# The first expert layer's weight splitting moved into the cross attention; bias two tiles ahead on GpSimd, context copies on ScalarE

## The chip, the cores and the metric

One Trainium2 chip, one of its cores. The metric is the device time of one execution in microseconds (us), the median of several; the profile is one further execution, recorded by the hardware profiler. The engines: TensorE (PE in the rows, its weight loads PEld), VectorE (DVE), ScalarE (ACT), GpSimd (POOL) and SyncE (SP), which issues DMAs.

## The reference, cut to what matters

```python
# two layers over x of 32 x 64 tokens, width 256; the change touches two steps of the first
x = x + L0_attn(layernorm(x), ...)                    # rotary recurrence
x = x + L0_xattn(layernorm(x), ctx, ctx, mask, ...)   # cross attention
x = x + L0_ffn(layernorm(x), ...)                     # 16 routed experts, top 2, and 2 shared
x = x + L1_attn(...); x = x + L1_xattn(...); x = x + L1_ffn(...)

def L0_xattn(query, key, value, mask, Wq, Wk, Wv, Wo):       # 16 heads of 16, 4 kv heads
    scores = einsum(Q / 4, K) + slope * (k - q)
    scores = where(mask, scores, finfo.min)
    return softmax(scores) @ V @ Wo

def L0_ffn(x, wa, rg, rgb, rw1, rb1, rw2, rb2, sg, sgb, sw1, sb1, sw2, sb2):
    aff = sigmoid(x @ wa); p, i = top_k(aff, 2); p = p / sum(p)
    expert(e) = (gelu(x @ g[e] + gb[e]) * (x @ w1[e] + b1[e])) @ w2[e] + b2[e]
    return x + sum over the 2 chosen of p * expert_r + sum over both shared of expert_s
```

## The kernel before, in words

The program is a row of stages, each an instruction block with a barrier at its end: load, rotary recurrence, cross attention, first experts, lightning attention, quantised attention, second experts. Within a block the order of each engine's instructions is written out by hand, and semaphores join them.

**Cross attention** (`gqa_cross_attention`, tag b). 2048 tokens are 16 tiles of 128, in 4 groups of 4 (a hardware loop `Fori(0, NBLK)`). A group begins with the projections of its 512 tokens: TensorE makes Q (L721) in two banks and K (L725), ScalarE copies them out (QT L604, Kbd L607), TensorE makes V from `ctxS` (L733), a copy of the group's context rows that GpSimd made with `tensor_copy` (L591); ScalarE copies V out (L613). Then for each tile: TensorE scores (L697); VectorE's `front`: scores times 1/4 plus bias (L651, two halves), row maximum (L656), subtract it (L657); ScalarE exp (L624); VectorE row sum (L672) and reciprocal (L673), then the front of the next tile; TensorE transposes (L745), ScalarE copies them out (PT L627), TensorE mixes V (L755); VectorE scales by the reciprocal (ao L677); TensorE transposes ao (L707), ScalarE copies it (aoT L618, `ao_copy`), TensorE multiplies by Wo (L715), VectorE adds to X (L662). GpSimd makes the `bias` of tile n, alibi plus mask (L595), in two buffers. `biased` starts at 2, so tiles 0 and 1 are made at once; the bias of tile n + 2 waits for the front of tile n to have read its buffer, and the next group's ctxS stands between.

**First experts** (`experts_top2`, tag c). TensorE works in fp16 pairs: each of the 18 experts' weights, scaled by 1024, is split in a high and a low half. SP loads gate, up (128x512 together) and down (128x256) of an expert into one of 6 staging slots (L1177, L1179; six experts ahead of the constants, two between the transposes, the rest when slots come free), ScalarE scales in place (L1256, L1257) and rounds to the high half (L1259, L1260), GpSimd subtracts for the low half (L1230, L1231). Beside it the layernorm runs (`RowNorm`: bn_stats L875, square root on ScalarE L905, reciprocal L880, normalise L893, add to X L898, high half on ScalarE L909, low half on VectorE L885), SP transposes each of 4 blocks (L918) and keeps its rows in memory (L919), TensorE makes the router's logits, and VectorE the routing (`Dispatch`: L1007 to L1107: choice, positions, one-hot tables, the list of tokens by expert). GpSimd gathers the rows by that list (L1240), SP transposes them (L1207), TensorE runs the experts over 12 quads, then the two shared experts; results go to memory (`y_dram`) and GpSimd gathers them back (L1248) in 8 slots G, which VectorE adds to X (L1353). ScalarE's queue has two splits ahead of the square root, one after each block's high half, two ahead of the router's weights (L984), and ten after the scores; SP's has two weight loads ahead of block 2's transpose. A stage of its own (`m.stage()`) clears the semaphores at its end.

Of the kernel before, what the change touches and what calls it, by code (L numbers as in the profile page):

```python
# [530 lines left out]
def gqa_cross_attention(nc, m, w):  # L531
# [10 lines left out]
    with ExitStack() as own:  # L542
# [12 lines left out]
        neg = sb("neg", [P, NT, SEQ])  # L555
# [11 lines left out]
        def preload(sp):  # L567
            def load(dst, src):
                sp.dma_start(dst, src).then_inc(loaded, 16)
            with nc.allow_non_contiguous_dma("small weights, mask rows"):  # L570
# [9 lines left out]
                for b in range(2):  # L580
                    src = w["mask_BxS2_bf1"].rearrange("(t b) k -> b t k", b=2)[b]
                    load(mask8[b * SEQ:(b + 1) * SEQ, :, :], src.partition_broadcast(SEQ))

        layernorm(nc, m, preload)
        with nc.Block() as block:
            @block.gpsimd
            def _(pool):
                pool.wait_ge(prep, 1 + KC * C)
                with pool.Fori(0, NBLK) as i:
                    pool.wait_ge(proj, i * 4 + 4)  # L590
                    pool.tensor_copy(ctxS[:, :, :], m.ctxT[:, :, ds(i * BLK, BLK)]).then_inc(ctx_copied, 1)  # L591
                    for tt in range(TPB):
                        n = i * TPB + tt
                        pool.wait_ge(biased, n + 1)
                        pool.tensor_tensor(bias[:, tt % 2, :, :], alibi[:, :, :],  # L595
                                           neg[:, ds(n, 1), :].broadcast_to((P, NH, SEQ)), ALU.add).then_inc(bias_ready, 1)

            @block.scalar
            def _(act):
                act.wait_ge(prep, 1 + KC * C)  # L600
                with act.Fori(0, NBLK) as i:
                    for c in range(2):
# [18 lines left out]
                    for tt in range(TPB):  # L621
# [7 lines left out]
                        if tt:  # L629
                            ao_copy(n - 1)  # L630
                    ao_copy(i * TPB + TPB - 1)

            @block.vector
            def _(dve):
                dve.wait_ge(loaded, 16 * NLOAD)
                dve.tensor_scalar(neg[:, :, :], mask8[:, :, :], 1.0, FLT_MAX, ALU.subtract, ALU.mult).then_inc(prep, 1)
# [50 lines left out]
            def _(pe):  # L687
                pe.wait_ge(prep, 1 + KC * C)
# [421 lines left out]
def experts_top2(nc, m, w, rows_dram, y_dram):  # L1110
# [8 lines left out]
    ORDER = [*range(NE + SH)]  # L1119
    STAGES, GOT, TURNED, GSLOTS = 6, 2, 3, 8  # L1120
    HS = 256.0
    shared_steps = SH * NBLK
    (scaled, high, split, hhigh, hlow, loaded, gate_up, gated, hready, downs, summed, bias_high, bias_split, bias_moved, bias_clear,
     tables, table_in, evac_act, evac_dve, combined) = (m.sem(f"c_{n}") for n in (
        "scaled", "high", "split", "hhigh", "hlow", "loaded", "gate_up", "gelu", "h", "downs", "summed", "bias_high",
        "bias_split", "bias_moved", "bias_clear", "tables", "table_in", "evac_act", "evac_dve", "combined"))
    w_in = [m.sem(f"c_w{i}") for i in range(STAGES)]
# [4 lines left out]
    with ExitStack() as own:  # L1132
# [24 lines left out]
        src_r = {"Wg": w["L0_ffn_rg"], "Wu": w["L0_ffn_rw1"], "Wd": w["L0_ffn_rw2"]}  # L1157
        src_s = {"Wg": w["L0_ffn_sg"], "Wu": w["L0_ffn_sw1"], "Wd": w["L0_ffn_sw2"]}
# [6 lines left out]
        with nc.Block() as block:  # L1165
            @block.sync
            def _(sp):
# [3 lines left out]
                def weights(n):  # L1171
                    if n >= STAGES:
                        sp.wait_ge(split, n - STAGES + 1)
                    e, slot = ORDER[n], n % STAGES
                    src, e = (src_r, e) if e < NE else (src_s, e - NE)
                    for part, name in enumerate(("Wg", "Wu")):
                        sp.dma_start(Wgu[:, slot, :, part, :],  # L1177
                                     src[name][e].rearrange("(k p) f -> p k f", p=P)).then_inc(w_in[slot], 16)
# [1277 lines left out]
```

## Time and profile before

| | |
|---|---|
| median of 3 runs | 2751.41 us (2748.73 to 2751.82) |
| profiled execution, its own time | 2745.09 us |
| its span, first to last instruction | 2743.3 us |
| mean granted TensorE clock | 0.794 |
| busy in the span | PE 74%, DVE 63%, ACT 52%, POOL 37% |
| DMA | 135.44 MB, mean 49 GB/s |
| cross attention | about 277 to 476 us |
| first experts | about 476 to 707 us |

Rows in order of time have the start, the busy time, the engine, the line, the operation with output and inputs, and in brackets the engine's idle time before it and who ended that. Groups have the count, busy time and mean. A line's number is that of the kernel before. Granted clock is in parts of 2.4 GHz.

### The profile page before, as it was taken

To read this page: it belongs to the slowest core of one execution; us is meant where nothing else is said; L and a number is where in the kernel's file an instruction comes from. 1 tells how busy PE (TensorE), PEld (TensorE's weight loads), DVE (VectorE), ACT (ScalarE), POOL (GpSimd) and SP (SyncE) were. 2 spreads that over 40 slices of the span, in tenths; PEclk is the share of its full clock that TensorE was granted. 3 is DMA by queue.
4 is the path that set the end of the run, shared out by engine and by line. 5 is a ranking of instruction groups with operands and counts; after the bars stand their busy time and mean duration, and the time that the engine had idled before them with its cause. 6 is when DMAs were issued, how large, how long until landed. Compare 5 with 4: busy or idle time off the path is not lost. (4 is left out here: it accounts for less than half of the span.)

```text
span 2743.3 us, 44098 instructions
## 1 busy us (share of the span) xinstructions
PE 2041.8 (74%) x15822; PEld 1216.7 (44%) x15822; DVE 1739.4 (63%) x3149; ACT 1419.1 (52%) x1986; POOL 1017.3 (37%) x920
## 2 busy tenths in 40 slices
PE   6784777168499999999764466666666549999998
PEld 3332555056377777777554122222222334444444
DVE  5997465724533333333456899999999645666665
ACT  4562332522333333333232688888888416666664
POOL 0000221653332232223233788888888500101010
PEclk9996877589799999999877555555555559999999
DMA  2000000675100000000000456666566300000001
GB/s 92 0 0 20 1 0 9 159 175 134 52 20 20 19 10 19 19 19 10 24 0 0 77 106 107 108 107 107 108 107 107 58 18 18 17 26 17 26 17 40
DMA packets 374723, 135.44 MB, mean 49 GB/s; under 512 B 317549, under 2 KB 371525, under 8 KB 374597
## 3 DMA queue, kind: packets, MB, share of 16 engines
q1 hardware_dynamic: 370757, 123.27, 21.4%
q0 software_dynamic: 3840, 10.49, 1.6%
q8 instruction: 79, 1.29, 0.2%
q14 instruction: 47, 0.39, 0.0%
HBM read 47.69 MB, written 10.49 MB: 21 GB/s over the span
## 5 line engine op out<-in xcount | busy, mean ns | idle before, releaser
L2021 POOL CAST xnT<-xl 128x2048 bf16<-128x2048 uint8 x256 | 483.6, 1890 | 15.4
L2056 PE MATMUL psum<-e_KT,e_QT 48*128 48x512 bf16 x1024 | 264.8, 617 | 272.7 <-DVE ctxT L2089 125.3
L2089 DVE TENSOR_SCALAR_CACHE_REDUCE ctxT<-psum,e_nsq 128x1024 f32<-128x1024 f32 x256 | 314.7, 1282 | 11.8 <-PE psum L2056 10.1
L2089 DVE TENSOR_SCALAR_CACHE_REDUCE e_Smore<-psum,e_nsq 128x1024 f32<-128x1024 f32 x256 | 314.7, 1281 | 1.5
L2107 ACT ACTIVATE xh<-e_Smore,e_ebias 128x2048 uint8<-128x2048 f32 x128 | 256.3, 2002 | 48.6 <-POOL e_ebias L2028 48.6
L2107 ACT ACTIVATE xh<-ctxT,e_ebias 128x2048 uint8<-128x2048 f32 x128 | 256.2, 2002 | 47.6 <-POOL e_ebias L2028 47.6
L1569 POOL TENSOR_TENSOR d_sq<-d_oS 128x512 f32<-128x512 f32 x64 | 99.1, 1549 | 420.8 <-ACT d_oS L1613 420.8
L117 PE MATMUL psum<-xh,d_WT 128*128 128x512 f16 x768 | 229.9, 382 | 2.6 <-DVE d_WT L1644 2.6
L2056 PEld LDWEIGHTS psum<-e_KT,e_QT 48*128 48x128 bf16 x1024 | 33.7, 107 | 402.6 <-DVE ctxT L2089 190.6
L1663 DVE TENSOR_TENSOR d_ACC<-psum,d_ACC 128x512 f32<-128x512 f32 x128 | 82.4, 686 | 171.1 <-PE psum L1717 171.1
L2245 POOL TENSOR_TENSOR f_WA<-f_W,f_WA 128x512 f16<-128x512 f32 x17 | 19.6, 1155 | 410.0 <-ACT f_W2H L2265 410.0
L2066 PEld LDWEIGHTS psum<-e_Vi,xnT 128*128 128x128 bf16 x4096 | 119.4, 104 | 112.1 <-issue 104.3
L117 PE MATMUL psum<-xh,f_WA 128*128 128x512 f16 x544 | 154.4, 387 | 13.9 <-DVEq L2300 11.8
L2316 DVE SCALAR_TENSOR_TENSOR X<-psum,f_route,X 128x256 f32<-128x256 f32 x272 | 112.8, 477 | 70.3 <-PE psum L2376 70.3
L2376 PE MATMUL psum<-f_W2H,f_hh 128*128 128x256 f16 x544 | 151.1, 278 | 3.1 <-DVE f_hh L2328 3.1
L2376 PE MATMUL psum<-f_W2L,f_hh 128*128 128x256 f16 (+1 forms) x544 | 150.8, 277 | 0.0
L2066 PE MATMUL psum<-e_Vi,xnT 128*128 128x16 bf16 x4096 | 131.2, 175 | 7.4 <-POOL xnT L2021 7.4
L1657 DVE SCALAR_TENSOR_TENSOR d_y<-d_gt,d_oS 128x512 f32<-128x512 f32 x64 | 44.3, 693 | 145.6 <-ACT d_oS L1613 145.6
L1717 PE MATMUL psum<-d_WoT,d_y 128*128 128x256 f32 x512 | 122.7, 382 | 5.8 <-DVE d_y L1657 5.7
L2279 ACT ACTIVATE f_h<-psum 128x512 f32<-128x512 f32 x68 | 40.6, 597 | 158.8 <-PE psum L117 158.8
L1597 ACT ACTIVATE d_kT<-psum 128x512 f32<-128x512 f32 x64 | 38.2, 597 | 159.3 <-PE psum L117 159.3
L2306 DVE TENSOR_TENSOR f_pr<-psum,f_h 128x512 f32<-128x512 f32 x68 | 47.0, 692 | 111.3 <-ACT f_h L2279 111.3
(364 smaller groups left out, 4682.3 us busy)
## 6 DMA issues: line engine op xcount, KB each, us to landing
kept_y<-c_y SPq DMA_DIRECT2D x12, 512.0 KB, 5.1
d_Wn<-in_L_attn_w_qkv SPq DMA_DIRECT2D x16, 384.0 KB, 3.2
f_W<-in_L_ffn_w_routed SPq DMA_DIRECT2D x32, 176.0 KB, 2.5
xl<-xh SPq DMA_TRANSPOSE x256, 3.0
ctx_rows<-in_ctx SPq DMA_DIRECT2D x1, 2048.0 KB, 8.5
X<-in_x SPq DMA_DIRECT2D x1, 2048.0 KB, 14.0
c_Wgu<-in_L_ffn_rg SPq DMA_DIRECT2D x16, 128.0 KB, 2.7
c_Wgu<-in_L_ffn_rw SPq DMA_DIRECT2D x16, 128.0 KB, 2.8
```

What stands on the lines that cost most here:

```text
L117: mm = pe.matmul(out, lhsT(a, k), rhs(b, k), start=(n == 0), stop=(n == len(terms) - 1))
L1569: pool.tensor_tensor(sq[:, :], o, o, ALU.mult).then_inc(squared, 1)
L1663: last = dve.tensor_tensor(a2, m.bank[6 + half][:, :], a2, ALU.add)
L1717: mm = pe.matmul(m.bank[6 + j // 2][:, (j % 2) * D:(j % 2 + 1) * D], y[:, j * P:(j + 1) * P], WoT[:, slot, :], start=True, stop=True)
L2021: pool.tensor_copy(PT[:, sl, :], P8[:, sl, :, :].rearrange("p c q -> p (c q)").bitcast(U8)).then_inc(unpacked, 1)
L2056: mm = pe.matmul(m.bank[pair_banks(c + odd) + q], QT[rows, n // 2, :], KTt[rows, n % H // 2, col:col + BLK], start=True, stop=True)
L2066: mm = pe.matmul(m.bank[6 + j // 8][:, j % 8 * HD:(j % 8 + 1) * HD], PT[:, n % SLOTS, k // 2 * 2 * P + k % 2:(k // 2 + 1) * 2 * P:2], Vi[: ...
L2089: dve.tensor_scalar(S32[sl][:, hf * HALF:(hf + 1) * HALF].rearrange("p (a b) -> p a b", a=2), m.psum[:, b:b + 2, :], nsq[:, n + odd:n + od ...
L2107: act.activation(e8[:, sl, :], S32[sl], ACT.Exp, bias=ebias[:, sl:sl + 1], scale=-1.0, accum_out=esum[:, n:n + 1]).then_inc(exped, 1)
L2306: dve.tensor_tensor(pr[:, st % 2, 0, :], m.bank[1][:, :], h1[:, st % 2, 0, :], ALU.mult).then_inc(product, 1)
L2316: last = dve.scalar_tensor_tensor(m.X[:, t, :], m.bank[4 + 2 * (q % 2) + j // 2][:, (j % 2) * D:(j % 2 + 1) * D], R.route[:, t, ds(e, 1)], ...
L2376: mm = pe.matmul(m.bank[4 + 2 * (q % 2) + j // 2][:, (j % 2) * D:(j % 2 + 1) * D], a, b, start=(n == 0), stop=(n == len(terms) - 1))
```

## The change

The buffers for staging (4 slots in place of 6) and for the split weights belong to a new class, `SplitWeights`, that lives over both stages, which now share one `m.stage()`. In the attention: the shared experts are loaded with the preload and split ahead of the first group; then one routed expert's split goes with each tile, on ScalarE after the tile's evacuations, on GpSimd ahead of the bias of the tile after the next. GpSimd's bias is made two tiles ahead across groups too (`neg` gets two zero rows for the last two), and its copy of the context goes to ScalarE, ahead of the first QT copy. In the expert stage all loads and splits are gone; the router's weights are rounded after block 0's high half, and the results are gathered in 16 slots laid over xnT.

```diff
+class SplitWeights:
+    NE, SH, F, SLOTS = 16, 2, 128, 4
...
+    def load(self, sp, kind, e, slot):
+        for part, name in enumerate(("g", "w1")):
+            sp.dma_start(self.Wgu[:, slot, :, part, :],
+                         self.w[f"L0_ffn_{kind}{name}"][e].rearrange("(k p) f -> p k f", p=P)).then_inc(self.w_in[slot], 16)
+        sp.dma_start(self.Wd[:, slot, :], self.w[f"L0_ffn_{kind}w2"][e]).then_inc(self.w_in[slot], 16)
+    def scalar(self, act, e, slot, loads, n):
+        act.wait_ge(self.w_in[slot], 48 * loads)
+        act.activation(self.Wgu[:, slot], self.Wgu[:, slot], ACT.Copy, scale=SPLIT)
+        act.activation(self.Wd[:, slot], self.Wd[:, slot], ACT.Copy, scale=SPLIT).then_inc(self.scaled, 1)
+        act.wait_ge(self.scaled, n + 1)
+        act.activation(self.Wx[:, ds(e, 1), 0].rearrange("p o k a f -> p (o k a f)"),
+                       self.Wgu[:, slot].rearrange("p k a f -> p (k a f)"), ACT.Copy)
+        act.activation(self.WdH[:, ds(e, 1)].rearrange("p o d -> p (o d)"), self.Wd[:, slot], ACT.Copy).then_inc(self.high, 1)
+    def gpsimd(self, pool, e, slot, n):
+        pool.wait_ge(self.high, n + 1)
+        flat = lambda x: self.Wx[:, ds(e, 1), x].rearrange("p o k a f -> p (o k a f)")
+        pool.tensor_tensor(flat(1), self.Wgu[:, slot].rearrange("p k a f -> p (k a f)"), flat(0), ALU.subtract)
+        pool.tensor_tensor(self.WdL[:, ds(e, 1)].rearrange("p o d -> p (o d)"), self.Wd[:, slot],
+                           self.WdH[:, ds(e, 1)].rearrange("p o d -> p (o d)"), ALU.subtract).then_inc(self.split, 1)
...
-        neg = sb("neg", [P, NT, SEQ])
+        neg = sb("neg", [P, NT + 2, SEQ])
...
+            for slot in range(W.SH):
+                W.load(sp, "s", slot, slot)
...
+            @block.sync
+            def _(sp):
+                for slot in range(W.SH):
+                    sp.wait_ge(W.split, slot + 1)
+                    W.load(sp, "r", slot, slot)
+                for slot in range(W.SH, W.SLOTS):
+                    W.load(sp, "r", slot, slot)
+                with sp.Fori(1, NBLK) as i:
+                    for slot in range(W.SLOTS):
+                        sp.wait_ge(W.split, i * W.SLOTS + (W.SH - W.SLOTS + 1) + slot)
+                        W.load(sp, "r", i * W.SLOTS + slot, slot)
             @block.gpsimd
             def _(pool):
+                for slot in range(W.SH):
+                    W.gpsimd(pool, W.NE + slot, slot, slot)
...
+                def mask_bias(n, half):
+                    pool.wait_ge(biased, n + 1)
+                    pool.tensor_tensor(bias[:, half, :, :], alibi[:, :, :],
+                                       neg[:, ds(n, 1), :].broadcast_to((P, NH, SEQ)), ALU.add).then_inc(bias_ready, 1)
+                mask_bias(0, 0)
+                mask_bias(1, 1)
                 with pool.Fori(0, NBLK) as i:
-                    pool.wait_ge(proj, i * 4 + 4)
-                    pool.tensor_copy(ctxS[:, :, :], m.ctxT[:, :, ds(i * BLK, BLK)]).then_inc(ctx_copied, 1)
                     for tt in range(TPB):
-                        n = i * TPB + tt
-                        pool.wait_ge(biased, n + 1)
-                        pool.tensor_tensor(bias[:, tt % 2, :, :], alibi[:, :, :],
-                                           neg[:, ds(n, 1), :].broadcast_to((P, NH, SEQ)), ALU.add).then_inc(bias_ready, 1)
+                        W.gpsimd(pool, i * W.SLOTS + tt, tt, i * W.SLOTS + (W.SH + tt))
+                        mask_bias(i * TPB + (tt + 2), tt % 2)
             @block.scalar
             def _(act):
+                for slot in range(W.SH):
+                    W.scalar(act, W.NE + slot, slot, 1, slot)
...
                 with act.Fori(0, NBLK) as i:
+                    act.wait_ge(proj, i * 4 + 4)
+                    act.activation(ctxS[:, :, :], m.ctxT[:, :, ds(i * BLK, BLK)], ACT.Copy).then_inc(ctx_copied, 1)
...
                         if tt:
                             ao_copy(n - 1)
+                        W.scalar(act, i * W.SLOTS + tt, tt, i + (2 if tt < W.SH else 1), i * W.SLOTS + (W.SH + tt))
                     ao_copy(i * TPB + TPB - 1)
...
-    STAGES, GOT, TURNED, GSLOTS = 6, 2, 3, 8
+    GOT, TURNED, GSLOTS = 2, 3, 16
...
-        G = norm.xn[:, :, :, :].rearrange("p a b d -> p (a b) d")
+        G = m.xnT[:, :, :].rearrange("p a b -> p (a b)").rearrange("p (s d) -> p s d", s=GSLOTS)
...
-                    for n in range(STAGES):
-                        weights(n)
...
-                    if b == 1:
-                        weights(STAGES)
-                        weights(STAGES + 1)
-                for n in range(STAGES + 2, NE + SH):
-                    weights(n)
...
-                for n in range(NE + SH):
-                    e, slot = ORDER[n], n % STAGES
-                    pool.wait_ge(high, n + 1)
-                    pool.tensor_tensor(Wx[:, e, 1], Wgu[:, slot], Wx[:, e, 0], ALU.subtract)
-                    pool.tensor_tensor(WdL[:, e], Wd[:, slot], WdH[:, e], ALU.subtract).then_inc(split, 1)
...
-                split_high(0)
-                split_high(1)
                 norm.scalar_sd(act)
-                for b in range(NBLK):
-                    norm.scalar_high(act, b)
-                    split_high(2 + b)
-                split_high(STAGES)
-                split_high(STAGES + 1)
+                norm.scalar_high(act, 0)
                 act.wait_ge(loaded, 16 * NLOADS)
                 act.activation(b2[:, 0, :], b2[:, 0, :], ACT.Copy, scale=HS * SPLIT).then_inc(bias_high, 1)
                 R.scalar_gate(act, R.wa[:, :, :].rearrange("p k e -> p (k e)"))
+                for b in range(1, NBLK):
+                    norm.scalar_high(act, b)
                 R.scalar_scores(act, m.bank[6])
-                for n in range(STAGES + 2, NE + SH):
-                    split_high(n)
...
-                pe.wait_ge(split, NE + SH)
...
-        with m.stage():
-            experts_top2(nc, m, w, kept_rows, kept_y)
+        with m.stage(), ExitStack() as split:
+            W = SplitWeights(m, w, split)
+            gqa_cross_attention(nc, m, w, W)
+            experts_top2(nc, m, w, W, kept_rows, kept_y)
```

## Rows read from the trace of the kernel before

**Rows 1.** Busy time (count) of stretches: length, PE, PEld, DVE, ACT, POOL, granted clock, DMA share, GB/s.
```profile
291.00:340.00 49.00, 36.87 (x324) 27.17 (x324) 28.04 (x32) 15.67 (x25) 11.39 (x5) 0.79 0.00 1
...
476.00:562.00 86.00, 8.05 (x164) 7.18 (x164) 58.70 (x150) 40.20 (x83) 53.99 (x46) 0.51 0.60 152
```

**Rows 2.** Timeline of the first group of the attention, VectorE and GpSimd.
```profile
293.38 2.31 DVE L657 TENSOR_TENSOR b_S<-b_S,b_mx 128x1024 f32<-128x1024 f32 x1
...
299.98 2.36 POOL L595 TENSOR_TENSOR b_bias<-b_alibi,b_neg 128x1024 f32<-128x1024 f32 x1 [5.37 <-DVE b_S L651]
...
301.09 2.33 DVE L657 TENSOR_TENSOR b_S<-b_S,b_mx 128x1024 f32<-128x1024 f32 x1
```

**Rows 3.** Timeline of the attention's last group, VectorE.
```profile
441.41 2.32 DVE L657 TENSOR_TENSOR b_S<-b_S,b_mx 128x1024 f32<-128x1024 f32 x1
...
456.70 1.23 DVE L657 TENSOR_TENSOR b_S<-b_S,b_mx 128x1024 f32<-128x1024 f32 x1
...
463.17 1.22 DVE L657 TENSOR_TENSOR b_S<-b_S,b_mx 128x1024 f32<-128x1024 f32 x1
```

**Rows 4.** Timeline, ScalarE's idle stretches in a tile and between groups.
```profile
313.87 0.39 ACT L618 ACTIVATE b_aoT<-psum 128x256 f32<-128x256 f32 x1
...
318.67 1.06 ACT L624 ACTIVATE b_S<-b_S 128x1024 f32<-128x1024 f32 x1 [4.40 <-DVE b_S L657]
...
332.18 0.60 ACT L604 ACTIVATE b_QT<-psum 128x512 f32<-128x512 f32 x1 [3.14 <-PE psum L721]
...
335.50 2.00 PEld L733 LDWEIGHTS psum<-b_Wv,b_ctxS 128*64 128x64 f32 x64 [0.76 <-issue]
```

**Rows 5.** GpSimd's subtractions by tile, ns min/median/max; ScalarE's splits in the timeline.
```profile
L1230 POOL TENSOR_TENSOR c_Wx<-c_Wgu,c_Wx x18: 1148/1188/3195, 481.9 to 544.5; 128x512 f16<-128x512 f32 x18
...
L1231 POOL TENSOR_TENSOR c_WdL<-c_Wd,c_WdH x18: 661/675/2717, 483.0 to 546.3; 128x256 f16<-128x256 f32 x18
...
521.13 0.61 ACT L1256 ACTIVATE c_Wgu<-c_Wgu 128x512 f32<-128x512 f32 x1
...
522.93 0.62 ACT L1256 ACTIVATE c_Wgu<-c_Wgu 128x512 f32<-128x512 f32 x1
```

**Rows 6.** Head of the experts to the logits: timeline, and groups by line.
```profile
485.25 0.25 DVE L880 RECIPROCAL c_rstd<-c_sd 128x16 f32<-128x16 f32 x1 [2.82 <-ACT c_sd L905]
...
485.54 1.38 DVE L893 TENSOR_SCALAR c_xn<-X,c_mom,c_rstd 128x256 f32<-128x256 f32 x4
...
L893 DVE TENSOR_SCALAR c_xn<-X,c_mom,c_rstd 128x256 f32<-128x256 f32 x16 | 8.1, 569 | 0.1
...
L885 DVE SCALAR_TENSOR_TENSOR xnT<-c_xn,xnT 128x1024 f16<-128x1024 f32 x4 | 5.7, 1458 | 0.0
...
508.66 3.54 SPq L918 DMA_TRANSPOSE xl<-xnT  x1
...
514.91 0.81 PE L117 MATMUL psum<-c_wa,xl 128*128 128x16 f16 x24 [1.75 <-DMA xl<-xnT]
```

**Rows 7.** Routing: groups by line, a short one of the later experts, the first gather.
```profile
L1053 DVE TENSOR_TENSOR c_base<-c_upto,c_need 128x16 f32<-128x16 f32 x1 | 1.1, 1120 | 0.0
...
L1089 DVE TENSOR_TENSOR c_tilehot<-c_iota,c_tile 128x768 f16<-128x768 f32 x2 | 3.3, 1633 | 0.0
...
L1091 DVE TENSOR_TENSOR c_tilehot<-c_tilehot,c_tokid 128x768 f16<-128x768 f16 x2 | 3.1, 1549 | 0.1
...
L1093 DVE TENSOR_TENSOR c_y<-c_iota,c_row 128x2048 f16<-128x2048 f32 x2 | 6.0, 2992 | 0.0
...
L828 DVE TENSOR_SCALAR f_tot<-f_tot 128x16 f32<-128x16 f32 x1 | 0.2, 175 | 0.0
...
549.16 1.30 POOL L1240 DMA_INDIRECT xnT<-kept_rows,c_token  x1 [2.20 <-DVE c_token L1107]
```

**Rows 8.** End of the stage: the last gather, the next stage's first instruction.
```profile
703.22 0.95 POOL L1248 DMA_INDIRECT c_xn<-kept_y,c_home  x1 [0.30 <-issue]
...
711.93 0.06 DVE L183 MEMSET ln_eps<- 128x1 f32 x1 [5.47 <-PEq L87]
```

More of the change, by code:

```diff
@@ L528, in _, with __init__, gqa_cross_attention @@
                 output(NBLK - 1)
-def gqa_cross_attention(nc, m, w):
+class SplitWeights:
+    NE, SH, F, SLOTS = 16, 2, 128, 4
+    def __init__(self, m, w, own):
+        NE, SH, F, SLOTS = self.NE, self.SH, self.F, self.SLOTS
+        self.w = w
+        self.Wgu = m.sb("c_Wgu", [P, SLOTS, KC, 2, F], ctx=own)
+        self.Wd = m.sb("c_Wd", [F, SLOTS, D], ctx=own)
+        self.Wx = m.sb("c_Wx", [P, NE + SH, 2, KC, 2, F], F16, own)
+        self.WdH, self.WdL = (m.sb("c_" + n, [F, NE + SH, D], F16, own) for n in ("WdH", "WdL"))
+        self.scaled, self.high, self.split = (m.sem(f"c_{n}") for n in ("scaled", "high", "split"))
+        self.w_in = [m.sem(f"c_w{i}") for i in range(SLOTS)]
+    def load(self, sp, kind, e, slot):
[17 more added lines that the diff above has]
+                           self.WdH[:, ds(e, 1)].rearrange("p o d -> p (o d)"), ALU.subtract).then_inc(self.split, 1)
+def gqa_cross_attention(nc, m, w, W):
     G, C, HD = 4, 4, 16
@@ L635, in _ @@
                 dve.wait_ge(loaded, 16 * NLOAD)
-                dve.tensor_scalar(neg[:, :, :], mask8[:, :, :], 1.0, FLT_MAX, ALU.subtract, ALU.mult).then_inc(prep, 1)
+                dve.memset(neg[:, NT:, :], 0.0).then_inc(prep, 1)
+                dve.tensor_scalar(neg[:, 0:NT, :], mask8[:, :, :], 1.0, FLT_MAX, ALU.subtract, ALU.mult).then_inc(prep, 1)
                 for k in range(KC):
@@ L1169, in load @@
                     sp.dma_start(dst, src).then_inc(loaded, 16)
-                def weights(n):
-                    if n >= STAGES:
-                        sp.wait_ge(split, n - STAGES + 1)
-                    e, slot = ORDER[n], n % STAGES
[L1175 to L1178, printed above, removed]
-                    sp.dma_start(Wd[:, slot, :], src["Wd"][e]).then_inc(w_in[slot], 16)
                 with nc.allow_non_contiguous_dma("biases to partitions"):
                     load(R.wa[:, :, :], w["L0_ffn_wa"].rearrange("(k p) e -> p k e", p=P))
-                    for n in range(STAGES):
-                        weights(n)
                     R.constants(load, w)
@@ L1252, in _ @@
             def _(act):
-                def split_high(n):
-                    e, slot = ORDER[n], n % STAGES
-                    act.wait_ge(w_in[slot], 48 * (n // STAGES + 1))
-                    act.activation(Wgu[:, slot], Wgu[:, slot], ACT.Copy, scale=SPLIT)
-                    act.activation(Wd[:, slot], Wd[:, slot], ACT.Copy, scale=SPLIT).then_inc(scaled, 1)
-                    act.wait_ge(scaled, n + 1)
-                    act.activation(Wx[:, e, 0], Wgu[:, slot], ACT.Copy)
-                    act.activation(WdH[:, e], Wd[:, slot], ACT.Copy).then_inc(high, 1)
                 def hidden_high(s):
```

23 lines of the change are left out of this document (7 added, 16 removed).

## The prediction

> **What bounds the kernel now.** I read the busy shares by stage first, then the instructions in order of time of the two stages that the change touches. The cross attention (277 to 476 us) runs in four groups of four tiles. In one group VectorE is busy 28 of 49 us, ScalarE 16, GpSimd 11 and TensorE 37 [rows 1]; no engine is full, it is a chain: scores, front (L651, L656, L657), exp, sum, next front. The head of the expert stage (476 to 562 us) has TensorE at 8 us of 86, VectorE at 59, GpSimd at 54 [rows 1]. It ends with the gather of the first rows; at its first instruction, 549.16, GpSimd had been idle for 2.20 us and waited for VectorE's list of tokens (c_token) [rows 7]. So VectorE's routing chain sets that stage, not the weights' splitting; what the splitting costs is what it does to VectorE, ScalarE's queue and SP's.
>
> That cost can be read. In the attention L657 takes 2.31 to 2.33 us where GpSimd's bias (2.36 us) began 1.1 us ahead of it, and ends 1.08 us after the bias ends [rows 2]; without one it takes 1.23 [rows 3]. VectorE stands still until GpSimd's instruction is over. Of the 16 L657, 14 are hit, all but the last two. In the other direction GpSimd's subtraction takes 1.15 us alone and up to 3.20 [rows 5].
>
> **The change, part by part.**
> Splitting in the attention, ScalarE: four activations a tile, 1.80 us from one split to the next [rows 5]. ScalarE has 4.40 us idle after the last evacuation of a tile, before the next exp [rows 4], so 1.8 is hidden, though 2.6 would be left of that cover before the exp is late; the faster tiles below take 1.1 off it again. After the fourth tile it has the tail of the group. The two shared experts' splits (3.6 us) stand ahead of the first group, where ScalarE waits for projections: 0, at most 1.
>
> ctxS by ScalarE: a copy of 128x1024, about the exp's 1.06 us [rows 4], ahead of the first QT evacuation, where ScalarE idles 3.14 us; it is done well before the V projection that needs it at 335.5, which comes 3.3 us after QT's start [rows 4]: 0. GpSimd loses four copies.
>
> SP: 18 x 3 loads move. In the loop each slot is loaded a group ahead (some 49 us), so no split waits for its load: 0. `neg` gains two rows and a memset: 0.1, left out.
>
> Bias: now behind GpSimd's two subtractions of the same tile, (1.19 + 0.68) + 2.35 = 4.2 us in one run, and these wait for ScalarE's split. Counted from L657's true start of tile n: exp, transposes, evacuations and the last copy end 4.4 to 5 us later (the copy of [rows 4] ends at 313.87 + 0.39; the exp before 318.67 was a tile of about 7.6 to 7.7 us earlier, 7.71 in [rows 2], so near 311.0; 3.2 from exp to copy, and 1.26 from L657 to exp; TensorE at its lower clock adds some), split 1.8 to 1.9, GpSimd 4.2, semaphores 0.2, and one wait of up to 1.1 behind the L657 in between. The bias of tile n+2 is there after 11.5 to 12.7 us. VectorE could use it after 2 x 6.47 - 2.6 = 10.3, with 6.47 the distance of two unhindered L657 [rows 3] and 2.6 the front's start ahead of its L657. So "two tiles ahead" is not quite reached: tiles 2 and 3 of a group wait for their bias. Followed step by step from L657 of tile 0: front of tile 2 at +12.1; L657 of tile 1 at +6.6; front of tile 3 12.7 after that; its exp 3.84 on: +23.1 to 23.2. Before, it is 318.67 - 293.38 = 25.3 [rows 2, 4]: 2.1 saved in each of three groups. The last group took 463.17 + 1.26 - 441.41 = 23.0 [rows 3]: 0.2 lost. Sum for the attention **-6.1**. Ends: 0, if L657 is caught as often as now, and about -12: a bias that is never late would give 3 x 6.47 + 1.26 = 20.7 a group and -16 in all, but then each L657 meets the first subtraction, which began just ahead of it, and about a quarter of that is lost.
>
> A rule is weighed here. [Rows 2] show a wait to the end of GpSimd's instruction. The Trainium skill, "SBUF — State Buffer", section "SBUF: two separate sides", says that VectorE with two SBUF inputs and a GpSimd operation that reads SBUF exclude each other, whoever starts first, for a whole instruction. The trace agrees (2.33 against 1.23). The rule speaks against this change, since GpSimd's time in a tile goes from 2.35 to 4.2 us; by it, with L657 falling anywhere in 7 us, a tile would wait (1.15² + 0.67² + 2.35²)/14 = 0.5 us on average, an estimate, against 1.1 now.
>
> Head of the experts, to the logits. ScalarE's first two splits leave: L880's idle 2.82 us [rows 6] falls to the square root's own 0.4, -2.4. The 16 normalisations are busy 8.1 us where four unhindered take 1.38 [rows 6], so 5.5: -2.6. The four L885 are busy 5.7 against 4 x 1.2 (as L657 alone): -0.9. The last of them then ends at 498.2 in place of 504.2. SP's queue has no weight loads between its transposes any more: block 2 is issued at 497.0, block 3 after the 2.1 to 3.5 that a transpose takes to issue and 0.6 to 1.0 for the rows, at 500.1 to 501.1. Now it is issued at 508.66 (3.54) and TensorE takes it at 514.91, 6.3 later [rows 6]; I let that be 4.3 to 6.3, since no weight load shares the queue. 504.4 to 507.3 against 514.9; I take **-9.2**, ends -7.6 and -10.5.
>
> Routing on VectorE. Two-input operations take 0.175 us at 16 elements (L828, where GpSimd is idle) and 1.22 at 1024, so about 0.96 at 768 and 2.28 at 2048. Rows now: L1089 1.63, L1091 1.55, L1093 2.99, two of each [rows 7]: 1.34 + 1.18 + 1.42; L1071, one of 768, gives 0.46 more. Eight short ones like L1053 (1.12, against 0.175) give 5.1 together. Sum **-9.5**; ends -5 (half of it is dependent latency) and -11.
>
> Tail: with 16 slots the gathers, one every 1.25 us, don't wait for a slot any more; the last comes 0.8 us earlier than 703.22 [rows 8]: **-0.8**. Stage boundary: 5.47 us now, with about 64 semaphores cleared [rows 8], then 89: 0 if as a range, +2.1 if one by one; nearest to the mix, **+0.5**. TensorE's later stages: granted clock 0.51 in the head [rows 1]; less time there costs it nothing I can find.
>
> Sum: -6.1 - 9.2 - 9.5 - 0.8 + 0.5 = **-25.1**. The profiled execution took 2745.09 us (span 2743.3), so 2720 for one like it; the median of before is 6.3 us above it, so 2751.41 - 25.1 = **2726.3 us**.
>
> **Rivals.**
> A, the contention moves along (0.14): GpSimd's runs meet L657 again in every tile, and some of VectorE's long routing times are not GpSimd's doing. For: 4.2 us a tile. Against: the run starts after ScalarE's split, when L657 of the next tile mostly has begun. Attention +2 (the last two tiles now hit too), routing -5: about -12, 2739.
> B, the bias chain becomes the bound (0.04), the slower side. Place: the front's wait for bias_ready in tiles 2 and 3. If the subtractions take their worst 3.20 and 2.72 [rows 5] each time, GpSimd's part grows 4.1 us: 2 x 4 x 4.1 = +33 against the sum, +8 in all, 2759. It decides from 3.8 us more per waiting tile (25.1 + 5.5 over 8). Against: those worst cases came where VectorE ran one two-input operation after another; in the attention it has one in a tile.
> C, larger (0.08): the bias is hardly late, transposes land early, the routing shrinks by 11: -12 - 10.5 - 11 - 0.8 = -34.3, near 2717.
> D, the change does not do what it says (in B and the forecast): the bias isn't really two ahead; priced above.
>
> **How the numbers follow.** Forecast 0.74. 0.2% is 5.5 us, about what can be told from no change. Faster: forecast, C and nearly all of A: 0.92; within: 0.04 (A's end, B's mild half); slower 0.04. Range: upper end A's -12 to -13, 2738.5; lower end C's -34, 2717.
>
> **What would show it.** L657 near 1.2 in tile 0 and 1; VectorE idle ahead of L651 in tiles 2 and 3, released by GpSimd's bias, 1 to 2 us; first exp to last exp of a group near 22. ScalarE's exp not late. L880's idle under 0.5; logits at about 29 us after the stage's start, in place of 39; L1053 near 0.18, L1093 near 2.3; gather 54 us after the stage's start in place of 73. Wrong if L657 stays at 2.3, if exps wait for a split, if L1053 stays near 1.1 with GpSimd idle, or if the head shrinks by under 12.

## The result, and the profile after

| | before | after |
|---|---|---|
| median | 2751.05 us (2748.73 to 2751.82, 4 runs) | 2727.1 us (2725.5 to 2728.46, 4 runs) |
| profiled execution, its own time | 2745.09 | 2728.19 |
| its span | 2743.3 | 2726.4 |
| mean granted TensorE clock | 0.794 | 0.795 |

The ratio is 0.9914, with a 95% interval of 0.9897 to 0.9931: 24 us less. The forecast was 2726.3 in a range of 2717 to 2738.5. The two profiled executions differ by only 16.9 us, so the stages have to be laid side by side. This table is worked out from the timelines, in us; bias_after_shift_b is bias_after_shift once more. The attention runs from the first instruction on `neg` to the load of the router's weights; the logits from there to the first MAX8; the routing from there to the copy of c_token; the quads from the first matmul of an expert to the first gather back; the gathers from the first to the last; the boundary from there to the first memset of the next stage.

| kernel | attention | logits | routing | quads | gathers | boundary | later stages |
|---|---|---|---|---|---|---|---|
| before | 198.6 | 40.4 | 31.9 | 101.4 | 39.5 | 8.7 | 2031.4 |
| after | 191.6 | 32.0 | 22.8 | 108.0 | 39.5 | 8.9 | 2030.7 |
| before_again | 198.7 | 39.9 | 31.7 | 104.7 | 39.5 | 8.7 | 2031.1 |
| again | 191.7 | 32.0 | 22.8 | 105.7 | 39.5 | 8.9 | 2029.1 |
| slots8 | 191.6 | 32.0 | 22.8 | 102.1 | 39.5 | 8.8 | 2026.5 |
| loads_back | 191.7 | 35.5 | 22.9 | 99.7 | 39.5 | 8.9 | 2032.4 |
| no_subtract | 198.6 | 44.4 | 22.8 | 102.4 | 39.5 | 8.7 | 2027.6 |
| bias_only | 201.8 | 40.8 | 31.7 | 106.5 | 39.5 | 8.7 | 2031.8 |
| shift_alone | 174.7 | 40.0 | 31.9 | 102.6 | 39.5 | 8.7 | 2032.6 |
| bias_first | 180.0 | 32.2 | 22.8 | 102.9 | 39.5 | 8.9 | 2029.9 |
| bias_after_shift | 174.7 | 32.1 | 22.8 | 102.4 | 39.6 | 8.9 | 2032.4 |
| bias_after_shift_b | 174.7 | 32.1 | 22.8 | 104.3 | 39.5 | 8.9 | 2030.6 |

Three stages changed, and each keeps its length to 0.5 us in every execution of the same code: attention -7.0, logits -8.4, routing -9.1, with +0.2 at the boundary 24.3 us less; the medians differ by 24.0. Two stretches are in no column and don't follow the change: what lies ahead of the attention (276.0 to 279.3 us over the kernels of the table) and from the list of tokens to the first expert (14.3 to 14.7 us). The quads and the later stages scatter over the rows of the table by some 8 and 6 us; the two profiled executions happened to stand 6.6 us apart in the quads, the wrong way for the change.

The answers to [rows 1], by stretches of the kernel after (length, PE, PEld, DVE, ACT, POOL busy with counts, granted clock, DMA share, GB/s):

```profile
290.00:339.00 49.00, 37.66 (x356) 27.28 (x356) 27.97 (x36) 23.93 (x44) 17.86 (x12) 0.82 0.12 34
470.00:539.00 69.00, 8.22 (x164) 7.26 (x164) 43.91 (x151) 8.04 (x11) 11.87 (x10) 0.51 0.37 87
```

The splitting stands in the attention now (ScalarE 15.7 to 23.9, GpSimd 11.4 to 17.9) and has left the head of the experts, where VectorE is busy 44 us in place of 59 for the same computation.

The answer to [rows 2, 4], the timeline of two tiles in the attention's second group, VectorE, ScalarE and GpSimd:

```profile
344.75 1.23 DVE L726 TENSOR_TENSOR b_S<-b_S,b_mx 128x1024 f32<-128x1024 f32 x1
345.20 1.79 POOL L569 TENSOR_TENSOR c_Wx<-c_Wgu,c_Wx 128x512 f32 x1 [17.73 <-ACT c_WdH L563]
346.95 0.67 POOL L570 TENSOR_TENSOR c_WdL<-c_Wd,c_WdH 128x256 f32 x1
347.58 2.36 POOL L651 TENSOR_TENSOR b_bias<-b_alibi,b_neg 128x1024 f32<-128x1024 f32 x1
350.07 1.29 DVE L720 SCALAR_TENSOR_TENSOR b_S<-psum,b_bias 128x512 f32<-128x512 f32 x2 [1.46 <-POOL b_bias L651]
352.10 0.40 ACT L563 ACTIVATE c_WdH<-c_Wd 128x256 f32 x1
352.65 1.22 DVE L726 TENSOR_TENSOR b_S<-b_S,b_mx 128x1024 f32<-128x1024 f32 x1
352.77 2.12 POOL L569 TENSOR_TENSOR c_Wx<-c_Wgu,c_Wx 128x512 f32 x1 [2.83 <-ACT c_WdH L563]
355.49 2.36 POOL L651 TENSOR_TENSOR b_bias<-b_alibi,b_neg 128x1024 f32<-128x1024 f32 x1
357.98 1.29 DVE L720 SCALAR_TENSOR_TENSOR b_S<-psum,b_bias 128x512 f32<-128x512 f32 x2 [1.47 <-POOL b_bias L651]
360.55 1.47 DVE L726 TENSOR_TENSOR b_S<-b_S,b_mx 128x1024 f32<-128x1024 f32 x1
362.06 1.06 ACT L691 ACTIVATE b_S<-b_S 128x1024 f32<-128x1024 f32 x1 [3.10 <-DVE b_S L726]
```

The row-max subtraction (L726, before L657) takes 1.2 us in place of 2.33 in 12 of the 16 tiles; it takes 1.88 in the second tile of the first group and 1.47 in the last tile of each other group. The wait has come back in another place: VectorE's front (L720) stands idle 1.46 and 1.47 us for GpSimd's bias, which had to wait for the split. At 352.77 the roles are turned: VectorE began first, and it is GpSimd's subtraction that takes 2.12 in place of 1.15.

The answers to [rows 6, 7]: head and routing, groups by line, then in order of time the reciprocal, the transposes, the last router matmul and the first gather:

```profile
L962 DVE TENSOR_SCALAR c_xn<-X,c_mom,c_rstd 128x256 f32<-128x256 f32 x16 | 5.5, 409 | 0.1
L954 DVE SCALAR_TENSOR_TENSOR xnT<-c_xn,xnT 128x1024 f16<-128x1024 f32 x4 | 4.8, 1218 | 0.0
L1162 DVE TENSOR_TENSOR c_y<-c_iota,c_row 128x2048 f16<-128x2048 f32 x2 | 4.6, 2285 | 0.0
L1160 DVE TENSOR_TENSOR c_tilehot<-c_tilehot,c_tokid 128x768 f16<-128x768 f16 x2 | 1.9, 958 | 0.1
L1158 DVE TENSOR_TENSOR c_tilehot<-c_iota,c_tile 128x768 f16<-128x768 f32 x2 | 1.9, 956 | 0.0
L1122 DVE TENSOR_TENSOR c_base<-c_upto,c_need 128x16 f32<-128x16 f32 x1 | 0.2, 176 | 0.0
```

```profile
476.86 0.25 DVE L949 RECIPROCAL c_rstd<-c_sd 128x16 f32<-128x16 f32 x1 [0.38 <-ACT c_sd L974]
483.51 2.06 SPq L987 DMA_TRANSPOSE xh<-xnT  x1
487.32 3.06 SPq L987 DMA_TRANSPOSE xh<-xnT  x1
491.13 3.48 SPq L987 DMA_TRANSPOSE xl<-xnT  x1
495.29 3.55 SPq L987 DMA_TRANSPOSE xl<-xnT  x1
500.65 0.81 PE L117 MATMUL psum<-c_wa,xl 128*128 128x16 f16 x24 [3.34 <-DMA xl<-xnT]
525.84 1.30 POOL L1280 DMA_INDIRECT xnT<-kept_rows,c_token  x1 [51.88 <-DVE c_token L1176]
```

Every operation of VectorE is back at its unhindered price: the 16 normalisations 8.1 to 5.5, the 2048-element product 2.99 to 2.29, the 16-element one (L1122, before L1053) 1.12 to 0.18. GpSimd had been idle for 51.88 us when it began on the list of tokens; in the kernel before it had waited 2.20 [rows 7].

The answer to [rows 8], the last gather and the next stage's first instruction:

```profile
686.72 0.94 POOL L1288 DMA_INDIRECT xnT<-kept_y,c_home  x1 [0.30 <-issue]
695.62 0.06 DVE L183 MEMSET ln_eps<- 128x1 f32 x1
```

### The profile page after: what moved, and what is told of

The parts are those of the page before. It is cut to its first block and busy times, and to the rows that moved or that the text cites. A ratio compares the mean times of both kernels' runs of the same rounds, so it can differ in the third digit from the quotient of the medians.

```text
span 2726.4 us, 44230 instructions
## 1 busy us (share of the span) xinstructions
PE 2041.7 (75%) x15822; PEld 1218.4 (45%) x15822; DVE 1710.8 (63%) x3150; ACT 1423.7 (52%) x1990; POOL 1014.1 (37%) x918
## 5 line engine op out<-in xcount | busy, mean ns | idle before, releaser
L2113 DVE TENSOR_SCALAR_CACHE_REDUCE ctxT<-psum,e_nsq 128x1024 f32<-128x1024 f32 x256 | 314.7, 1282 | 11.4 <-PE psum L2080 10.1
L569 POOL TENSOR_TENSOR c_Wx<-c_Wgu,c_Wx 128x512 f32 (+1 forms) x18 | 26.0, 1443 | 384.3 <-ACT c_WdH L563 384.3
```

Of the source, the lines that this page charges most:

```text
L2113: dve.tensor_scalar(S32[sl][:, hf * HALF:(hf + 1) * HALF].rearrange("p (a b) -> p a b", a=2), m.psum[:, b:b + 2, :], nsq[:, n + odd:n + od ...
```

## The experiments

**again**: the kernel after, unchanged, to see what the quads do in another execution.

> The changed kernel once more, as the yardstick of this set. In the first profile the routed experts' quads (first expert matmul to the first gather of results) took 108.0 us where the profile of before had 101.4, which gave back 6.6 of the 23.3 us won by then, although the medians stand 24 us apart. Theory 1: the quads' length varies from execution to execution (DMA transposes and gathers), and the change does nothing there; then this profile shows the quads somewhere between 101 and 108 us, and the ratio is 0.991 (24 to 25 us). Theory 2: the change lengthens the quads by 6 to 7 us each time; then this profile shows 107 to 109 again.

Measured: 2724.6 us (median of 6), ratio 0.9913, interval 0.9898 to 0.9927. Attention, logits and routing repeat to 0.1 us, the quads took 105.7 in place of 108.0. Over all kernels of the table they lie between 99.7 and 108.0.

**before_again**: the kernel before, unchanged.

> The kernel before once more, for its profile. If the quads' length varies by itself, they take another time than the 101.4 us of the first profile; the median of before is 6 us above that first profiled execution, so I expect about 107. If the length belongs to the kernel, 101 to 102 again.

Measured, in a single execution: 2749.79 us, quads 104.7, which is neither the 107 that I expected nor 101.4 again. The five profiles with the splitting in the routing have a mean of 103.5 us of quads, the seven with it in the attention 103.6. So the difference in the quads is scatter and no cost of the change; which transfer makes it was not tried.

**bias_only**: the kernel before with the bias two tiles ahead and the context copied by ScalarE. The splitting stays in the routing.

```diff
...
+                mask_bias(0, 0)
+                mask_bias(1, 1)
                 with pool.Fori(0, NBLK) as i:
-                    pool.wait_ge(proj, i * 4 + 4)
-                    pool.tensor_copy(ctxS[:, :, :], m.ctxT[:, :, ds(i * BLK, BLK)]).then_inc(ctx_copied, 1)
                     for tt in range(TPB):
-                        n = i * TPB + tt
-                        pool.wait_ge(biased, n + 1)
-                        pool.tensor_tensor(bias[:, tt % 2, :, :], alibi[:, :, :],
-                                           neg[:, ds(n, 1), :].broadcast_to((P, NH, SEQ)), ALU.add).then_inc(bias_ready, 1)
+                        mask_bias(i * TPB + (tt + 2), tt % 2)
...
                 with act.Fori(0, NBLK) as i:
+                    act.wait_ge(proj, i * 4 + 4)
+                    act.activation(ctxS[:, :, :], m.ctxT[:, :, ds(i * BLK, BLK)], ACT.Copy).then_inc(ctx_copied, 1)
...
```

> Kernel before with only the attention's part of the change that is not splitting: bias two tiles ahead across groups, context rows by ScalarE. The bias of tile n+2 still starts when the front of tile n has read its buffer, 1.1 us ahead of L657. Theory 1 (mine now: the attention's gain comes from the subtractions, which push the bias away from the row-maximum subtraction): all 16 of these VectorE instructions take 2.3 us, two more than before; attention 2 us longer, no gain at all, 0 to +2 us in all. Rival (the prediction's title reading: making the bias ahead is what gains): the attention shrinks by 6 to 7 us, 2744 us.

Measured: 2752.74 us against 2748.15 for the kernel before beside it, ratio 1.0016, interval 1.0007 to 1.0025. Its subtraction, all 16 (count, then ns min/median/max):

```profile
L663 DVE TENSOR_TENSOR b_S<-b_S,b_mx x16: 2314/2328/2350, 293.4 to 464.3; 128x1024 f32<-128x1024 f32 x16
```

Before, two of 16 went free; now none, and the attention takes 3.2 us more: 2.2 in the last group's tiles, and 1.0 behind its last exp, where the granted clock is 0.59 in place of 0.70. The bias "two tiles ahead" gives nothing by itself: what matters here is not how early it is ready but when it starts. It starts when the front has read the buffer, 1.1 us ahead of the subtraction, and holds it to its end. The three longer stretches between the groups keep their lengths to 0.04 us although ScalarE now copies the context rows in them, so that copy costs nothing.

**bias_after_shift**: the kernel after, but GpSimd's bias waits for the row-max subtraction that VectorE has in hand (`shifted`), and the weights' subtractions stand behind it, one tile later.

```diff
                     for tt in range(TPB):
-                        W.gpsimd(pool, i * W.SLOTS + tt, tt, i * W.SLOTS + (W.SH + tt))
+                        pool.wait_ge(shifted, i * TPB + (tt + 1))
                         mask_bias(i * TPB + (tt + 2), tt % 2)
+                        if tt:
+                            W.gpsimd(pool, i * W.SLOTS + (tt - 1), tt - 1, i * W.SLOTS + (W.SH + tt - 1))
+                    W.gpsimd(pool, i * W.SLOTS + (TPB - 1), TPB - 1, i * W.SLOTS + (W.SH + TPB - 1))
```

> Changed kernel, but GpSimd makes the bias of tile n+2 as soon as tile n's row maximum has been subtracted (wait on shifted), and takes the weights' subtractions of the tile before after it. Theory 1 (the lock and the late bias are all that is left in the tiles): no such VectorE instruction above 1.3 us, VectorE never waits for the bias (9.2 us in 7 waits in the changed kernel), tiles 6.5 us apart; attention 8 to 11 us shorter than in the changed kernel, about 2717 us. Rival 1 (ScalarE's split or TensorE's slow clock takes over as the bound at 7.5 us a tile): 2 to 4 us. Rival 2: the subtractions now meet VectorE each tile: 0 or slower.

Measured: 2707.81 us (2705.68 to 2710.17), ratio 0.9856, interval 0.9839 to 0.9872. The attention is 16.9 us shorter than in the kernel after, and not 8 to 11: 11.3 of them lie in the tiles, which is what the theory was about, and 5.6 between the groups, where I expected nothing. And once more, in another set:

> The same kernel as bias_after_shift, a second time, beside shift_alone on the same chip. Theory: the same 2706 to 2710 us, 174.7 us of attention, 22.8 of routing, and 25 to 30 us less than shift_alone. If the lower time was a draw of the first experts' loads, it comes out above 2715.

Measured: 2705.07 us (2700.82 to 2705.69), ratio 0.9838, interval 0.9823 to 0.9853. The time repeats; the distance to shift_alone is 19.9 us and not 25 to 30, since shift_alone came out faster than I had thought. The kernel beats both others, the one after by 16.8 us where the two ran in one set (2724.6 in **again**). The timeline of its first tiles, from the first set:

```profile
294.11 1.22 DVE L729 TENSOR_TENSOR b_S<-b_S,b_mx 128x1024 f32<-128x1024 f32 x1
295.63 2.37 POOL L651 TENSOR_TENSOR b_bias<-b_alibi,b_neg 128x1024 f32<-128x1024 f32 x1 [7.62 <-DVE b_S L729]
298.15 1.29 DVE L723 SCALAR_TENSOR_TENSOR b_S<-psum,b_bias 128x512 f32<-128x512 f32 x2 [0.19 <-POOL b_bias L651]
300.73 1.23 DVE L729 TENSOR_TENSOR b_S<-b_S,b_mx 128x1024 f32<-128x1024 f32 x1
302.22 2.38 POOL L651 TENSOR_TENSOR b_bias<-b_alibi,b_neg 128x1024 f32<-128x1024 f32 x1 [4.23 <-DVE b_S L729]
304.56 1.16 POOL L569 TENSOR_TENSOR c_Wx<-c_Wgu,c_Wx 128x512 f32 x1
```

GpSimd starts 0.3 us after the subtraction has ended, in the 2.3 us in which VectorE waits for the exp and sums from it, and the next front comes 6.6 us after the one before it. The subtraction for tile 0's weights starts at 304.56, behind the second bias, when VectorE reads its scores from PSUM.

**bias_first**: the same order on GpSimd, the bias ahead of the weights, but without the wait and without the delay by one tile.

```diff
                     for tt in range(TPB):
-                        W.gpsimd(pool, i * W.SLOTS + tt, tt, i * W.SLOTS + (W.SH + tt))
                         mask_bias(i * TPB + (tt + 2), tt % 2)
+                        W.gpsimd(pool, i * W.SLOTS + tt, tt, i * W.SLOTS + (W.SH + tt))
```

> Changed kernel with the bias of tile n+2 ahead of the subtractions of tile n in GpSimd's order. Theory 1 (the bias starts 1.1 us ahead of VectorE's subtraction again and holds it up): those instructions take 2.3 us in all 16 tiles, VectorE never waits for a bias; tiles 7.6 us apart as before, attention about 7 to 9 us longer than in the changed kernel, near 2735 us. Rival (the port is no matter, only the late bias is): the attention shrinks by the 9.2 us that VectorE waits for the bias now, 2718 us.

Measured: 2709.73 us, ratio 0.9859, interval 0.9842 to 0.9877; attention 180.0. I had expected a subtraction of 2.3 us in every tile, and it came in the first tile of each group alone (4 of 16; the maximum below is one of them):

```profile
L726 DVE TENSOR_TENSOR b_S<-b_S,b_mx x16: 1224/1226/2345, 292.6 to 446.6; 128x1024 f32<-128x1024 f32 x16
```

From the second tile on, the weights' subtractions of the tile before stand ahead of the bias in GpSimd's order, and they wait for ScalarE's split; so the bias starts when the row-max subtraction has passed, as if the wait stood there. My theory fell. Against bias_after_shift the attention is 5.3 us longer (180.0 - 174.7), but this is a sum of 8.2 more in the tiles and 2.9 less between the groups. Four hits of 1.1 us are 4.5 of the 8.2. Most of the rest is one tile of the third group, where the granted clock was 0.63 and VectorE waited 1.71 and 1.69 us for TensorE's products, so the 5.3 are not the price of the order alone.

**shift_alone**: bias_only with that one wait, the splitting untouched in the routing.

```diff
...
                     for tt in range(TPB):
+                        pool.wait_ge(shifted, i * TPB + (tt + 1))
                         mask_bias(i * TPB + (tt + 2), tt % 2)
...
```

> The splitting of the first layer's weights stays where the kernel before has it, in the routing; only the bias is made on GpSimd, two tiles ahead, and it waits for the row-max subtraction of the tile before. Theory (the lock between the two engines alone sets the attention): no row-max subtraction takes over 1.3 us, VectorE doesn't wait for a bias in the steady tiles, tiles stand 6.5 us apart, and the attention takes 12 to 20 us less than the 198.6 of the kernel before (the three tails that the other splitting filled included), with logits and routing unchanged at 40.4 and 31.9: 2731 to 2739 us. Rival (once the lock is gone, the bound is the chain over TensorE and ScalarE, which the kernel before already has): 4 to 6 us less, 2745 us. If the attention falls by more than 20, the splitting that bias_after_shift does in it costs it time, and the best place for the splitting would be looked for again.

Measured: 2724.95 us (2724.14 to 2726.34), ratio 0.9915, interval 0.9901 to 0.9928. Attention 174.7, which is 23.9 less than before: I had written 12 to 20, so the theory's mechanism holds and its number is missed by 4 us. My last sentence was wrong too. The attention fell by more than 20, yet with the splitting in it (bias_after_shift) it takes the same 174.7, so the splitting costs it nothing. In its timeline (VectorE and GpSimd) the tiles stand 6.6 and 6.5 us apart, as in bias_after_shift:

```profile
294.68 1.23 DVE L664 TENSOR_TENSOR b_S<-b_S,b_mx 128x1024 f32<-128x1024 f32 x1
296.20 2.36 POOL L592 TENSOR_TENSOR b_bias<-b_alibi,b_neg 128x1024 f32<-128x1024 f32 x1 [11.48 <-DVE b_S L664]
298.73 1.29 DVE L658 SCALAR_TENSOR_TENSOR b_S<-psum,b_bias 128x512 f32<-128x512 f32 x2 [0.19 <-POOL b_bias L592]
301.31 1.23 DVE L664 TENSOR_TENSOR b_S<-b_S,b_mx 128x1024 f32<-128x1024 f32 x1
```

bias_only and this kernel differ by the wait alone, and it is worth 27.1 us of attention: 16.8 inside the tiles, 10.3 between the groups. So the kernel before with the bias ahead and this wait is as fast as the changed kernel, and the two gains add up: 2752.7, with the wait 2725.0, with the rest of the change too 2705.1. The wait without the bias made ahead was not tried.

**no_subtract**: the kernel before, with GpSimd's subtractions in the routing left out. The low halves of the first experts' weights are zeroed at the stage's start instead, and are missing from its output.

```diff
+                pool.memset(Wx[:, :, 1].rearrange("p e k a f -> p e (k a f)"), 0.0).then_inc(bias_clear, 1)
+                pool.memset(WdL[:, :, :], 0.0).then_inc(bias_clear, 1)
...
-                    pool.tensor_tensor(Wx[:, e, 1], Wgu[:, slot], Wx[:, e, 0], ALU.subtract)
-                    pool.tensor_tensor(WdL[:, e], Wd[:, slot], WdH[:, e], ALU.subtract).then_inc(split, 1)
+                    pool.sem_inc(split, 1)
```

> Kernel before, but GpSimd doesn't subtract for the low halves of the first experts' weights (they are zeroed at the stage's start); ScalarE's splits and all loads stay. Theory 1 (GpSimd's subtractions are what stretches VectorE's routing): L1053 and its like fall from 1.1 to 0.2 us, L1093 from 3.0 to 2.3; scores to token list about 9 us shorter, normalisation about 3.5 shorter of which part is lost in SP's queue; the gather starts 10 to 12 us earlier, near 2740 us. Rival (the routing's long instructions have another cause, ScalarE's or the DMAs'): they stay, and the time is within 2 us of before.

Measured: 2742.29 us, ratio 0.9983, interval 0.9972 to 0.9993. The routing takes 22.8 us, that of the kernel after, while ScalarE's splits and the weights' loads still run beside it. So the gain in the routing is that of GpSimd's subtractions, and no part of it that of the loads or of ScalarE. The logits took 4.0 us longer than before, and the timeline of the head shows my own memsets there:

```profile
479.07 7.78 POOL L1227 MEMSET c_Wx<- 128x9216 f16 x1
484.74 0.25 DVE L880 RECIPROCAL c_rstd<-c_sd 128x16 f32<-128x16 f32 x1 [3.10 <-ACT c_sd L905]
485.03 6.62 DVE L893 TENSOR_SCALAR c_xn<-X,c_mom,c_rstd 128x256 f32<-128x256 f32 x4
486.79 4.08 POOL L1228 MEMSET c_WdL<- 128x4608 f16 x1
```

Four normalisations that take 1.38 us alone took 6.62. One by one in the trace, the first took 1.96 us and ended 0.14 us after the first memset did (486.85), the second took 4.10 and ended 0.14 after the second memset (490.87); the other two took their usual 0.4. A memset reads nothing, and still holds VectorE.

**loads_back**: the kernel after, with six weight loads (two experts, into buffers of their own) put back on SP's queue behind block 1's transpose, where the kernel before had them.

> Changed kernel with six weight loads (to a buffer of their own, not used) put back on SP's queue between the second and third of the stage's transposes. Theory 1 (SP's queue is the rest of the gain to the logits: the third block's transpose is ready when its rows are): the last transpose is issued 2.5 to 3.5 us later and the gather with it; +3 us. Rival (the loads' traffic rather than the queue makes the transposes slow): the last transpose lands 6.2 us or more after its issue and +4 to +6. Rival 2 (the queue had slack): 0.

Measured: 2727.63 us, ratio 0.9933, interval 0.9913 to 0.9953; logits 35.5 in place of 32.0. SP's queue (five of the six loads left out):

```profile
487.67 2.99 SPq L987 DMA_TRANSPOSE xh<-xnT  x1
490.70 0.59 SPq L988 DMA_DIRECT2D kept_rows<-xnT  x1
491.33 0.53 SPq L1247 DMA_DIRECT2D c_again<-in_L_ffn_rg  x1
...
495.00 3.37 SPq L987 DMA_TRANSPOSE xl<-xnT  x1
499.04 3.59 SPq L987 DMA_TRANSPOSE xl<-xnT  x1
```

The six issues occupy the queue from 491.33 to 495.00, and the last transpose comes 3.4 us later after its stage's start. TensorE takes it 5.4 us after its issue, as in the kernel after, so the queue is at work here and not the traffic. With all else as in the kernel after, these loads are worth 3.4 of the 8.4 us in the logits; the other 5.0 (VectorE's operations, ScalarE's two splits) have no run that parts them.

**slots8**: the kernel after with 8 gather slots in place of 16.

```diff
-    GOT, TURNED, GSLOTS = 2, 3, 16
+    GOT, TURNED, GSLOTS = 2, 3, 8
...
-        G = m.xnT[:, :, :].rearrange("p a b -> p (a b)").rearrange("p (s d) -> p s d", s=GSLOTS)
+        G = norm.xn[:, :, :, :].rearrange("p a b d -> p (a b) d")
```

> Changed kernel with 8 slots for the gathers back, in their old place. The prediction put 0.8 us on the 16 slots. In the changed kernel's first profile the gathers take 39.5 us from first to last, the same as before. Theory 1 (the last gather is bound by GpSimd's own pace and by what holds its descriptor writes up, not by slots): no difference, within 0.5 us. Rival: +0.8 us.

Measured: 2723.36 us, ratio 0.9916, interval 0.99 to 0.9931; 39.5 us of gathers with either, and the distances between the 32 gathers agree to 0.02 us. The slots are worth nothing.

## Why the prediction was right, and where it was not

The total, -25.1 forecast and -24.0 measured, came out because the logits and the routing were priced by their rows. The attention's part was right in its sum alone, and that is luck: its tiles gave 2.7 us less than forecast, and stretches that I had not counted gave 3.6.

- **Attention, -6.1; measured -7.0.** The mechanism was as told: of 14 hit subtractions 11 become free and three are held for 0.2 to 0.7 us, and from the second group on the bias of tiles 2 and 3 is late. In the second group: the front of tile 2 came 11.94 us after the subtraction of tile 0 (350.07 - 338.13; forecast 12.1). The front of tile 3 came 13.23 after the subtraction of tile 1 (357.98 - 344.75; forecast 12.7), since GpSimd's subtraction met VectorE's twice, 1.79 and 2.12. And the last subtraction took 1.47. From the front of tile 0 to the exp of tile 3 the four groups changed by -1.6, -1.4, -1.4 and +0.9, together -3.4, against the -6.1 of the sum. This term was mis-sized: 23.9 us for a group where I had 23.2. The first group has another course: its bias is late by 0.35 us only, but VectorE waits 1.70 us at 312.12 for TensorE's product with Wo (2.08 us there, 1.13 at 317.89; granted clock 0.68 in the group), and one exp starts 0.24 us late, behind ScalarE's split. Neither was in my sum.
- **What filled it up was no step of mine.** Between groups, -3.6: -4.1 in the first of the four stretches, +0.1 and -0.6 in the next two, +1.0 in the last. Two of them in the kernel after, from the last exp of a group to the next front, then the first one before:

```profile
318.10:335.50 17.40, 14.79 (x148) 9.86 (x147) 3.40 (x7) 11.26 (x20) 8.21 (x6) 1.00 0.17 46
362.10:383.20 21.10, 17.93 (x144) 12.69 (x144) 3.34 (x7) 11.32 (x19) 6.23 (x4) 0.76 0.13 37
```

```profile
318.70:340.20 21.50, 18.25 (x144) 12.52 (x144) 3.35 (x8) 8.44 (x14) 0.00 (x0) 0.76 0.00 1
```

  After the first group the granted clock was 1.00 (2.4 GHz throughout) in place of 0.76, and the same work took 17.4 us and not 21.5. I had treated these tails as fixed.
- **The lower end of -12 for the attention.** I argued that a bias never late would make each row-max subtraction meet GpSimd's first subtraction. No run has the change's order with a bias that is never late, so for this kernel the end stays untested; in another order it doesn't hold: bias_after_shift has -23.9, with 14.7 less in the tiles and 9.2 less in the tails. Rival C took its attention term from this end.
- **Lock against chance.** My estimate of 0.5 us a tile, with the instructions falling at random, was not what happened: they are tied to each other. The row-max subtractions were held 1.4 us in all 16 tiles, 0.09 a tile, always at the same places, and the late bias with its 1.46 to 1.48 us comes back in both tiles of the last three groups.
- **Logits, -9.2; measured -8.4.** Reciprocal's idle 2.82 to 0.38, normalisations 8.1 to 5.5, L954 (was L885) 5.7 to 4.8: each as forecast. The last transpose was issued 25.4 us after the stage's start (forecast 24.3 to 25.3) and taken 5.4 later (4.3 to 6.3). The third transpose takes 3.5 us to issue without any load beside it, the upper end of my 2.1 to 3.5; I had taken the middle. That is 0.6 of the missing 0.8.
- **Routing, -9.5; measured -9.1.** The long operations gave 1.35 + 1.18 + 1.41, L1071 0.47 and the eight short ones 5.1, each as forecast; no_subtract shows the cause. My price for a short two-input operation came from L828, which has one input; L1122, with two, took 0.176 all the same. Two operations of 256 elements gave 0.5 more, unpriced; VectorE's busy time fell by 10.0 us, and the stage by 9.1.
- **Tail, -0.8; measured 0.** This step failed: I read the gathers as held by slots, and no row showed that. Most come 1.25 us after the one before, of which 0.95 is the gather and 0.30 its issue, with 8 slots and with 16.
- **Boundary, +0.5; measured +0.2**, near the 0 of semaphores cleared as a range and far from the +2.1 of one by one.
- **ScalarE's splits, context copy and SP's loads in the attention, 0.** For the splits and loads shift_alone against bias_after_shift shows it, 174.7 us without the splitting and with it; for the copy bias_only. The two shared experts' splits ahead of the first group cost nothing: from the first instruction on `neg` to the first front it is 13.6 us before and after.
- **Rivals.** A fell with the free subtractions and the full gain in the routing; four of 16 tiles were met, for 1.4 us in all. B's bias made the front wait 1.5 us at most, where it decides from 3.8. C fell with the late bias. D was in the sum, and bias_only bears it out.

## What to carry to other kernels

When two engines shut each other out for whole instructions, as VectorE and GpSimd do here, look beyond their busy shares at which instruction starts just ahead of which. Look at what releases the longer one, and if it is released just ahead of the other engine's two-input operation, let it wait for that operation to end: here the bias made ahead and one wait on a semaphore that already existed gave 24 us, as much as the whole change. A producer made "further ahead" gains nothing if the same event still starts it. And before a result is explained by one pair of profiles, see in a second pair which stages scatter.

## What was not expected of the hardware

- GpSimd's memsets, which read nothing, stretched VectorE's `tensor_scalar` from 1.38 to 6.62 us for four, although it has one tensor for input. The Trainium skill, "SBUF — State Buffer", section "SBUF: two separate sides", has this too: an operation of VectorE in a mode that takes two ports excludes any operation of GpSimd. The trace agrees (6.62 against 1.38, and two of the four end 0.14 us after a memset); that these ran in such a mode no row says by itself. I had used the half of the rule on two inputs alone.
- What lies between the groups changes with the granted clock, though TensorE's work in it is the same. Three of the four tails in shift_alone, where the splitting does not stand in them:

```profile
315.50:335.80 20.30, 16.77 (x144) 11.70 (x144) 3.39 (x7) 9.49 (x15) 2.36 (x1) 0.83 0.00 1
403.50:420.90 17.40, 13.87 (x144) 9.39 (x144) 3.41 (x7) 9.49 (x15) 2.36 (x1) 1.00 0.00 0
444.70:453.20 8.50, 5.54 (x52) 4.44 (x52) 3.33 (x7) 2.76 (x5) 2.38 (x2) 1.00 0.00 0
```

  The last takes 8.5 us at full clock, 11.4 at 0.70 before and 12.4 at 0.59 after; the first is 21.5 at 0.76 before, 20.3 at 0.83 here. The 10.3 us between the groups that the wait of shift_alone gave are of this kind. Faster tiles alone don't explain it: in bias_first the third group is the slowest (27.6 us at 0.63), and its tail takes 17.4 at 1.00. Why the first group's tail runs at full clock in the kernel after, and the third's and fourth's in this one, stays open; no run varied it alone.
- In the kernel after, a DMA transpose on SP's queue takes 2.06 us to issue as the first, then 3.06, 3.48 and 3.55, with no load in the queue and only the store of each block's rows between them. Before, the four took 2.17, 1.98, 3.13 and 3.54. What sets it was not tried.
